# Landmark attention in one list of steps, and delta's first inverse on VectorE

## The chip, the cores and the metric

The kernel runs on one core of a Trainium2 chip. The metric is the device time of one execution, in microseconds (us).

## The reference

A decoder of two layers on x (4 batches, 512 tokens, 512 channels): delta-rule attention, a selective scan, a feed-forward with sign weights, landmark attention, cross attention with rotary positions, a feed-forward with ternary weights. After each comes `x = layernorm(x + f(x))`. The change is in the fourth, and at one place in the first. Landmark attention has 32 heads of 16 channels, eight blocks of 64 tokens, and 4 landmarks a block, 32 in all:

```python
q, k, v = split_heads(x @ w_qkv + b_qkv); q, k = rope(q), rope(k)
out_local = masked_softmax(qb @ kb * scale, causal) @ vb                # within each block of 64
lm = softmax(pool_q @ kb * scale) @ vb                                  # 4 landmarks per block
lm = lm + (masked_softmax(lq @ lk * scale, lm_mask) @ lv) @ w_lm_out    # lq, lk, lv = lm @ w_lm_qkv
lm = lm + (softmax((lm @ w_l2t_q) @ kb * scale) @ vb) @ w_l2t_out
gk, gv = lm @ w_lm_kv
out_global = masked_softmax(q @ gk * scale, g_mask) @ gv                # blocks before one's own
gate = sigmoid(x @ w_gate + b_gate)
out = ((1 - gate) * out_local + gate * out_global) @ w_out + b_out
```

In the delta rule each chunk of 32 tokens needs the inverse of a 32x32 unit triangular matrix for each head.

## The kernel before

Six stages run one after the other. Each has a class with a program for every engine: `pe_` TensorE, `act_` ScalarE, `dve_` VectorE, `pool_` GpSimd, `sp_` the queue of SyncE that issues most DMAs. The programs are in order and meet by semaphores. A stage starts when the stores of the one before have landed. A `Ring` hands out PSUM banks in a written order: TensorE fills a bank when the engine that read its last content has emptied it.

`Landmark` (line 1884) runs its four batches in a hardware loop, one turn each, with one set of buffers. All weights are loaded once, 3 MB of `wqkv` before the first product. A turn has four phases. The front: transposing x, the gate, v, q and k by token tile (`pe_project`, line 217), the rotation of q and k on VectorE (five operations each for q and k in each of four tiles, lines 2481 to 2491), and their transposes on TensorE (line 2215), copied by ScalarE. Then SyncE duplicates v into `VV` with 16 DMAs. The local phase: 16 items (c, t), eight heads and 128 tokens each, in the order of `local_order`. For an item GpSimd spreads the keys over eight masked copies `Kz` (line 2052), TensorE makes the scores (line 2237), VectorE adds the causal mask (line 2578), takes the maximum (2386) and subtracts it (2388), ScalarE takes exp (2349), VectorE sums (2498), TensorE transposes (2244), ScalarE copies, TensorE multiplies with v (2255). Between the items stand the 16 steps of the landmark `CHAIN`, whose small products, softmaxes and sums depend on each other. The global phase: eight items of 16 heads and 128 tokens against 32 landmark keys, the same way (lines 2267, 2637, 2366, 2608, 2274), and 32 narrow value products (line 2281); `mix` applies sums and gate on VectorE, and GpSimd scales the local part (2058). Output: 16 transposes (2289), the product with `wo` (224), residual, bias and normalization (2651 to 280), store. The next turn's x is loaded ahead, nothing else of it starts early.

`Delta` (line 343) works on eight pairs of batch and head half. For each, `pool_all` (line 531) inverts the triangles with 62 operations on GpSimd (lines 542 and 544), widths from 31 to 256, 10,912 columns in all, between the DMA that brings `p32` and the DMAs that carry the result to `DT`, which TensorE's triangle products wait for (line 623). Its ring has six banks; in its order V (two banks) stands six places before PT, the masked query product, and PT before the next pair's k products (line 606). GpSimd's operation for the next pair waits until the inverse before it is stored.

## Time and profile before

| what | value |
|---|---|
| median of 3 runs | 3782.99 us (3773.44 to 3783.01) |
| profiled execution: its own time, its span | 3802.12 us, 3800.4 us |
| busy in the span: TensorE, VectorE, ScalarE, GpSimd | 77%, 61%, 32%, 29% |
| mean granted clock of TensorE | 0.851 |
| landmark attention | 1943.1 to 2874.4 us, 931.3 us |

A row of a window gives its length, then for each engine its busy microseconds and, in brackets, its instructions; PEclk is TensorE's granted clock as a share of 2.4 GHz. PE is TensorE's products, PEld its weight loads, DVE VectorE, ACT ScalarE, POOL GpSimd. In a timeline a row is start, length, engine, source line, operation and shapes, with the idle time before it and what ended that. One f32 product shows as two records.

### The profile page before, as it was taken

Reading aid. Unit: us, or ns where it says so; the run is one execution under the profiler, and the core shown is the slowest. Engines: PE = TensorE matmul, PEld = TensorE weight load, DVE = VectorE, ACT = ScalarE, POOL = GpSimd, SP = SyncE. Lnnn points to the kernel's source line nnn. Section 1 sums busy time; section 2 is a strip of 40 time slices with the busy share of each in tenths; the row PEclk is TensorE's granted clock in tenths of the full one; section 3 lists DMA queues with packets and bytes.
Section 4 is the critical chain, followed back from the end, with each engine's and each line's share of the span. In section 5 each row is a group of like instructions: output and inputs, shape, how many; then the busy total and the mean of one; then the engine's idle time right before and its main releaser. Section 6 shows DMA issues by size and latency. Waiting matters only on the chain.

```text
span 3800.4 us, 53319 instructions
## 1 busy us (share of the span) xinstructions
PE 2924.6 (77%) x20710; PEld 1523.5 (40%) x20710; DVE 2317.4 (61%) x3434; ACT 1231.3 (32%) x2016; POOL 1104.5 (29%) x1044
## 2 busy tenths in 40 slices
PE   5788888765655655599968788878875798989877
PEld 4565656531222212244434545545452233333234
DVE  1233333327898989787727668575773565656567
ACT  3232323203434343211102212122121465645645
POOL 4433333305555555300002112020213442433000
PEclk8788988866877778899988788887887899999989
DMA  2222121103112120401050000000004543434211
GB/s 76 66 45 66 45 66 45 43 29 119 52 54 68 55 68 32 160 35 38 27 196 7 23 23 23 23 13 23 12 13 111 107 103 77 105 73 87 84 42 45
DMA packets 195820, 226.10 MB, mean 59 GB/s; under 512 B 99480, under 2 KB 131768, under 8 KB 194672
## 3 DMA queue, kind: packets, MB, share of 16 engines
q1 hardware_dynamic: 194480, 218.44, 20.4%
q0 software_dynamic: 1088, 4.19, 0.4%
q8 instruction: 171, 2.80, 0.3%
q14 instruction: 81, 0.66, 0.1%
HBM read 154.69 MB, written 54.92 MB: 55 GB/s over the span
## 4 chain that ended last, share of the span: by engine, by line
PE 39%; DVE 12%; issue 6%; ACT 3%; DMA 1%; SPq 0%; POOL 0%; DVEq 0%; ACTq 0%; POOLq 0%
PE ps L224 7%; PE ps L1726 4%; PE ps L1737 4%; PE ps L3007 3%; PE ps L2994 3%; PE ps L2980 2%; PE ps L2939 2%; PE ps L2971 2%; PE ps L2237 1%; DVE arena L2386 1%; PE ps L2281 1%; PE ps L2102 1%; DVE arena L1334 1%; PE ps L2255 1%; ACT arena L3085 1%
## 5 line engine op out<-in xcount | busy, mean ns | idle before, releaser
L3180 DVE TENSOR_REDUCE arena<-ps 128x1 f32<-128x512 f32 x512 | 330.7, 686 | 262.2 <-PE ps L2980 261.0
L224 PE MATMUL ps<-arena 128*128 128x512 f32 (+3 forms) x1296 | 478.2, 527 | 9.9 <-ACT arena L856 3.1
L1382 PE MATMUL ps<-arena 128*128 128x512 f32 x512 | 314.4, 759 | 129.9 <-POOL arena L1366 129.9
L1366 POOL TENSOR_TENSOR arena<-arena 128x1024 f32<-128x1024 f32 x128 | 309.6, 2419 | 299.3 <-DVE arena L1358 298.3
L3085 ACT ACTIVATE arena<-ps 128x512 f32<-128x512 f32 x512 | 288.1, 598 | 285.9 <-PE ps L2994 282.4
L1358 DVE TENSOR_TENSOR_SCAN arena<-ps,arena 128x1024 f32<-128x1024 f32 x128 | 291.7, 2280 | 64.2 <-ACT ps L1349 63.7
L2052 POOL TENSOR_TENSOR arena<-arena 128x1024 f32<-128x1024 f32 x64 | 127.3, 1994 | 605.5 <-ACT arena L2310 356.7
L224 PEld LDWEIGHTS ps<-arena 128*128 128x128 f32 (+2 forms) x1296 | 198.9, 157 | 255.9 <-issue 191.7
L542 POOL TENSOR_TENSOR arena<-arena 128x31 f32<-128x31 f32 (+15 forms) x248 | 149.0, 601 | 378.2 <-DMA arena<-d_a 359.4
L1382 PEld LDWEIGHTS ps<-arena 128*128 128x128 f32 x512 | 115.4, 239 | 320.7 <-POOL arena L1366 190.4
L1349 ACT ACTIVATE ps<-arena 128x511 f32<-128x511 f32 x256 | 165.2, 680 | 241.2 <-DVE arena L1358 241.0
L2994 PE MATMUL ps<-arena 99*128 99x512 bf16 x512 | 197.9, 389 | 54.4 <-ACT arena L3085 33.3
L2980 PE MATMUL ps<-arena 96*128 96x512 bf16 x512 | 199.1, 391 | 22.4 <-issue 18.1
L1726 PE MATMUL ps<-arena 128*128 128x512 bf16 x768 | 168.2, 381 | 7.7 <-issue 7.7
L1737 PE MATMUL ps<-arena 128*128 128x512 bf16 x768 | 166.9, 379 | 0.0
L1334 DVE TENSOR_TENSOR arena<-ps,arena 128x1024 f32<-128x1024 f32 x128 | 154.4, 1207 | 0.8
L1030 DVE TENSOR_TENSOR arena<-ps,arena 128x256 f32<-128x256 f32 x120 | 51.0, 425 | 165.4 <-PE ps L743 165.4
L3007 PE MATMUL ps<-arena 128*32 128x512 f32 x1024 | 141.6, 626 | 1.0 <-ACT arena L3085 1.0
L544 POOL TENSOR_TENSOR arena<-arena 128x31 f32<-128x31 f32 (+15 forms) x248 | 135.4, 546 | 19.4
L2994 PEld LDWEIGHTS ps<-arena 99*128 99x128 bf16 x512 | 49.5, 98 | 206.0 <-ACT arena L3085 142.9
L2878 POOL TENSOR_TENSOR arena<-arena 128x512 f32<-128x512 f32 x32 | 40.8, 1274 | 308.5 <-ACT arena L3058 308.5
L1378 PE MATMUL ps<-arena 128*128 128x512 f32 x32 | 32.6, 1123 | 114.2 <-DVE arena L1408 114.2
(337 smaller groups left out, 5421.7 us busy)
## 6 DMA issues: line engine op xcount, KB each, us to landing
arena<-d_bc SPq DMA_DIRECT2D x32, 1024.0 KB, 5.3
arena<-d_x SPq DMA_DIRECT2D x24, 1024.0 KB, 5.6
arena<-d_parts SPq DMA_DIRECT2D x192, 128.0 KB, 4.3
d_x<-arena SPq DMA_DIRECT2D x64, 256.0 KB, 2.5
d_parts<-arena SPq DMA_DIRECT2D x32, 384.0 KB, 2.4
arena<-arena SPq DMA_DIRECT2D x64, 128.0 KB, 2.0
d_w<-arena SPq DMA_DIRECT2D x3, 1408.0 KB, 4.8
arena<-d_w SPq DMA_DIRECT2D x3, 1408.0 KB, 11.2
```

The source lines that it names most:

```text
L224: ins = pe.e.matmul(ps[:m, :n], lhsT(k), rhs(k), start=(k == 0), stop=(k == chunks - 1))
L1334: dve.e.tensor_tensor(s.h[:, i % s.HS].rearrange("p (w l) -> p w l", w=s.W), spread(s.ps[:, s.DTU, :], 1, s.W), s.bc[:, turn % s.SLOTS, 0] ...
L1358: dve.e.tensor_tensor_scan(h, s.dA[:, i % 2].rearrange("p w l -> p (w l)"), h, 0.0, ALU.mult, ALU.add).then_inc(*dve.up("scan_scanned"))
L1366: pool.e.tensor_tensor(h, h, s.bc[:, turn % s.SLOTS, 1], ALU.mult).then_inc(*pool.up("scan_hC"))
L1382: ins = pe.e.matmul(y, s.ident, s.h[:, i % s.HS, w * L:(w + 1) * L], start=False, stop=last)
L1726: ins = e.matmul(ps, s.up[:, k, m * P:(m + 1) * P], s.xp[i][:, k, :], start=(k == i == 0), stop=(k == C - 1 and i == 2))
L1737: ins = e.matmul(ps, s.hp[i][:, m, t * P:(t + 1) * P], s.down[:, m, :], start=(m == i == 0), stop=(m == s.FC - 1 and i == 2))
L2980: pe.e.matmul(s.rmax.bank((u, m)), s.Qs[:s.N, slot, h, t * P:(t + 1) * P], s.Ks[:s.N, slot, h, :], start=True, stop=True).then_inc(*s.rmax ...
L2994: pe.e.matmul(s.rexp.bank((u, i)), s.Ks[:s.N + 3, slot, s.G * g + j, k * P:(k + 1) * P], s.Qs[:s.N + 3, slot, s.G * g + j, :], start=True, ...
L3007: ins = e.matmul(ps[32 * j:32 * j + 32, :], s.V[:, u % s.SLOTS, k, s.G * g + j, :], s.E[:, k % 2, j, :], start=(k == 0), stop=(k == s.KEYS ...
L3085: act.e.activation(s.E[:, k % 2, j], s.rexp.bank((u, i)), ACT.Exp).then_inc(*s.rexp.empty(act, (u, i)))
L3180: dve.e.tensor_reduce(s.mx[:, u % 2, t, h:h + 1], s.rmax.bank((u, m)), AX.X, ALU.max, negate=True).then_inc(*s.rmax.empty(dve, (u, m)))
```

## The change

The loop goes. `schedule` writes one list of steps for all four batches, and every engine's program walks that list: a first front; then for each batch 20 local steps, 11 global ones and four of output. Into the steps go the landmark chain, now 18 pieces, and the front of the next batch. v, QT, KT and the gates have two buffers, p has three. Weights other than wq and wk pass through three slots of 1 MB, loaded in the order of use.

q and k are computed transposed, 128 channels by 512 tokens (`r`), so that their transposes go. ScalarE adds the bias while copying; two DMAs swap neighbouring channels; GpSimd rotates with three operations of 512 columns. The local and global masks are bf16 products of an identity with the mask, accumulated under the scores, and VectorE's mask additions go. The masked keys are eight ScalarE copies of 128 columns an item, with a scale from memory. Sum and gate are applied to the exp before its transpose: VectorE makes a factor an item, GpSimd multiplies. The values are made transposed: v times the 64 transposed columns for the local part, eight products of 512 columns for the global part, added on VectorE; the output transposes go. v is duplicated whole by four DMAs of 512 KB, and GpSimd masks the pairs. In delta VectorE makes the inverse of the first pair; GpSimd keeps the other seven.

```diff
-        for n in range(s.PAIRS):
-            if n:
-                pool.e.wait_ge(*pool.on("delta_t32_out", n - 1))
+        for n in range(1, s.PAIRS):
+            pool.e.wait_ge(*pool.on("delta_t32_out", n - 1))
             e.tensor_tensor(s.t32, s.id32, s.id32, ALU.mult).then_inc(*pool.up_step("delta"))
             pool.e.wait_ge(*pool.on("delta_p32", n))
...
+    def dve_inverse(self, dve):
+        s, e, st = self, dve.e, "delta"
+        e.tensor_copy(s.t32, s.id32).then_inc(*dve.up_step(st))
+        dve.e.wait_ge(*dve.on("delta_p32", 0))
+        for j in range(s.Q - 1):
+            a, m = j + 1, s.Q - 1 - j
+            pr = s.prod[:, :a * m].rearrange("p (c i) -> p c i", i=m)
+            dve.e.wait_ge(*dve.at_step(st))
+            e.tensor_tensor(pr, spread(s.t32[:, :a, j], 2, m), spread(s.p32[:, a:, j], 1, a), ALU.mult).then_inc(*dve.up_step(st))
+            dve.e.wait_ge(*dve.at_step(st))
+            ins = e.tensor_tensor(s.t32[:, :a, a:], s.t32[:, :a, a:], pr, ALU.subtract)
+            if j < s.Q - 2:
+                ins.then_inc(*dve.up_step(st))
+            else:
+                ins.then_inc(*dve.up("delta_inverse"))
...
                     if i == 1:
                         s.dve_beta_k(dve, n)
+                        if n == 0:
+                            s.dve_inverse(dve)
...
+    CHAIN = ["pool_s", "pool_T", "pool_v", "lq", "lk", "lv", "ls", "lpT", "lo", "loT", "lout", "l2q",
+             "read_s", "read_T", "read_v", "rout", "gk", "gv"]
     SMALL = ["lq", "lk", "lout", "l2q", "rout", "gk"]
+    MATRICES = {"lq": ("D_wlm", 0), "lk": ("D_wlm", 1), "lv": ("D_wlm", 2), "v": ("D_wqkv", 2), "lout": ("D_wlo", 0), "l2q": ("D_wl2q", 0),
+                "rout": ("D_wl2o", 0), "gk": ("D_wkv", 0), "gv": ("D_wkv", 1), "y": ("D_wo", 0)}
+    TURNED = [(c, w) for w in (1, 0) for c in range(C)]
+    FIRST_FRONT = [[("xT", 0)], [("xT", 1)], [("xT", 2)], [("xT", 3)], [("r", 0)], [("r", 1)], [("r", 2)], [("r", 3)], [("r", 4), ("gateT", 0)],
+                   [("v", 0), ("gate", 0)], [("v", 1)], [("v", 2)], [("v", 3)]]
+    FIRST_LOCAL = {-2: [("r", 5)], -1: [("r", 6)], 0: [("r", 7)]}
+    LOCAL_FRONT = {2: [("xT", 0)], 3: [("xT", 1)], 4: [("xT", 2)], 5: [("xT", 3), ("gateT", 0)], 6: [("v", 0), ("gate", 0)], 7: [("v", 1)],
+                   8: [("v", 2)], 9: [("v", 3)], 11: [("r", 0)], 12: [("r", 1)], 13: [("r", 2)], 14: [("r", 3)]}
+    GLOBAL_FRONT = {-1: [("r", 4)], 2: [("r", 5)], 5: [("r", 6)], 8: [("r", 7)]}
...
+    def schedule(self):
+        s = self
+        fronts = lambda table, k, b: [(what, b, i) for what, i in table.get(k, [])] if b < B else []
+        for k, front in enumerate(s.FIRST_FRONT):
+            yield "front", -1, k, None, [(what, 0, i) for what, i in front]
+        for b in range(B):
+            for k in range(-2, s.N + 2):
+                first = fronts(s.FIRST_LOCAL, k, 0) if b == 0 else []
+                yield "local", b, k, s.CHAIN[k + 1] if 0 <= k + 1 < len(s.CHAIN) else None, first + fronts(s.LOCAL_FRONT, k, b + 1)
+            for k in range(-2, s.NG + 1):
+                yield "global", b, k, None, fronts(s.GLOBAL_FRONT, k, b + 1)
+            for t in range(T):
+                yield "out", b, t, None, []
...
+    def sp_vv(self, sp, b):
+        s = self
+        sp.e.wait_ge(*s.ring.at_emptied(sp, ("v", b, T - 1)))
+        if b:
+            sp.e.wait_ge(*s.ro.at_filled(sp, ("o", b - 1, C - 1)))
+        for half in range(2):
+            for b2 in range(2):
+                sp.e.dma_start(s.VV[64 * half:64 * half + 64].rearrange("p (t b) d -> p t b d", b=2)[:, :, b2, :],
+                               s.v[64 * b2:64 * b2 + 64, b % 2]).then_inc(*sp.up("landmark_vdup", 16))
...
+    def sp_swap(self, sp, b, r):
+        s, j = self, b * len(self.TURNED) + r
+        sp.e.wait_ge(*s.ring.at_emptied(sp, ("r", b, r)))
+        if j >= 2:
+            sp.e.wait_ge(*sp.on("landmark_rot", j - 2))
+        for odd in range(2):
+            sp.e.dma_start(s.sw[odd::2, j % 2], s.raw[1 - odd::2, j % 2]).then_inc(*sp.up(f"landmark_swapped{j % 2}", 16))
...
+    def pool_scale(self, pool, b, i):
+        s, j = self, b * self.N + i
+        pool.e.wait_ge(*pool.on("landmark_factor", j))
+        p = s.p[:, i % 3].rearrange("p (h n) -> p h n", n=s.S)
+        pool.e.tensor_tensor(p, p, spread(s.ls[:, i % 3], 2, s.S), ALU.mult).then_inc(*pool.up("landmark_scaled"))
...
+    def pool_rope(self, pool, b, r):
+        s, e, j = self, pool.e, b * len(self.TURNED) + r
+        c, w = s.TURNED[r]
+        if j == 0:
+            pool.e.wait_ge(*pool.at_all("landmark_rope"))
+        pool.e.wait_ge(*s.ring.at_emptied(pool, ("r", b, r)))
+        if j:
+            pool.e.wait_ge(*pool.on("landmark_rot", j - 1))
+        e.tensor_tensor(s.m1, s.raw[:, j % 2], s.cos, ALU.mult).then_inc(*pool.up("landmark_cos"))
+        pool.e.wait_ge(*pool.on(f"landmark_swapped{j % 2}", j // 2))
+        e.tensor_tensor(s.sw[:, j % 2], s.sw[:, j % 2], s.sin, ALU.mult).then_inc(*pool.up("landmark_sin"))
+        pool.e.wait_ge(*pool.on("landmark_cos", j))
+        pool.e.wait_ge(*pool.on("landmark_sin", j))
+        if b >= 2 and r == 0:
+            pool.e.wait_ge(*s.ring.at_filled(pool, ("gs", b - 2, s.NG - 1)))
+        e.tensor_tensor((s.QT, s.KT)[w][:, b % 2, c], s.m1, s.sw[:, j % 2], ALU.add).then_inc(*pool.up("landmark_rot"))
...
+    def pool_all(self, pool):
+        s = self
+        turned = []
+        for phase, b, k, chain, front in s.steps:
+            if phase == "local":
+                if s.item(k + 1) is not None:
+                    s.pool_scale(pool, b, k + 1)
+            if phase == "global" and s.item(k + 1, s.NG) is not None:
+                s.pool_g_scale(pool, b, k + 1)
+            for fb, r in turned:
+                s.pool_rope(pool, fb, r)
+            turned = [(fb, r) for what, fb, r in front if what == "r"]
+            if phase == "local" and b == 0 and -1 <= k < T - 1:
+                for i in range(2):
+                    s.pool_pairs(pool, 0, 2 * (k + 1) + i)
+            if phase == "global" and k >= s.NG - 3 and b + 1 < B:
+                for i in range(2):
...
+    def pe_scores(self, pe, b, i):
+        s, e, R = self, pe.e, self.ring
+        c, t = divmod(i, T)
+        if t == 0:
+            pe.e.wait_ge(*pe.on("landmark_rot", b * len(s.TURNED) + C + c))
+        if b == i == 0:
+            pe.e.wait_ge(*pe.at_all("landmark_masks"))
+        pe.e.wait_ge(*pe.on("landmark_kz", b * s.N + i))
+        pe.e.wait_ge(*R.at_free(pe, ("s", b, i)))
+        ps = R.bank(("s", b, i)).rearrange("p (h k) -> p h k", h=s.HC)
+        for b2 in range(2):
+            at = t * P + 64 * b2
+            e.matmul(ps[64 * b2:64 * b2 + 64], s.identb[:, 64 * b2:64 * b2 + 64], spread(s.m_local, 1, s.HC), start=True, stop=False)
+            ins = e.matmul(ps[64 * b2:64 * b2 + 64], s.QT[:, b % 2, c, at:at + 64], s.Kz[:, i % 2, :, 64 * b2:64 * b2 + 64], start=False, stop=True)
+        ins.then_inc(*R.fill(pe, ("s", b, i)))
...
+    def pe_global(self, pe, b, k):
+        s, e, R = self, pe.e, self.ring
+        i = s.item(k + 2, s.NG)
+        if i is not None:
+            half, t = divmod(i, T)
+            if i == 0:
+                pe.e.wait_ge(*pe.on("landmark_kz2", b, 2))
+            pe.e.wait_ge(*R.at_free(pe, ("gs", b, i)))
+            ps = R.bank(("gs", b, i)).rearrange("p (c n) -> p c n", c=2)
+            for c in range(2):
+                e.matmul(ps[:, c, :].rearrange("p (h n) -> p h n", n=s.NL), s.identb, spread(s.m_gl[:, t], 1, s.HC), start=True, stop=False)
+                ins = e.matmul(ps[:, c, :], s.QT[:, b % 2, 2 * half + c, t * P:(t + 1) * P],
+                               s.kz[:, 2 * half + c].rearrange("p h n -> p (h n)"), start=False, stop=True)
+            ins.then_inc(*R.fill(pe, ("gs", b, i)))
...
+    def act_kz(self, act, b, i):
+        s = self
+        c, t = divmod(i, T)
+        if t == 0:
+            act.e.wait_ge(*act.on("landmark_rot", b * len(s.TURNED) + c))
+        if i >= 2:
+            act.e.wait_ge(*s.ring.at_filled(act, ("s", b, i - 2)))
+        elif b:
+            act.e.wait_ge(*s.ring.at_filled(act, ("go", b - 1, C - 1)))
+        for h in range(s.HC):
+            act.e.activation(s.Kz[:, i % 2, h], s.KT[:, b % 2, c, t * P:(t + 1) * P], ACT.Copy, scale=s.bm16[:, h:h + 1]).then_inc(*act.up("landmark_kz"))
...
+    def act_all(self, act):
+        s = self
+        for phase, b, k, chain, front in s.steps:
+            if (phase, k, b) == ("local", -2, 0) or phase == "out" and k == 1 and b + 1 < B:
+                s.act_kz(act, b if phase == "local" else b + 1, 0)
+                s.act_kz(act, b if phase == "local" else b + 1, 1)
+            if phase == "local" and k >= -1 and s.item(k + 3) is not None:
+                s.act_kz(act, b, k + 3)
+            if phase == "local":
+                if k == -2 and b:
+                    s.act_sqrt(act, b - 1)
+                if s.item(k) is not None:
+                    s.act_turned(act, b, k)
+                if s.item(k + 2) is not None:
+                    s.act_exp(act, b, k + 2)
+                if k >= 1 and (k - 1) % T == T - 1:
+                    s.act_out(act, b, (k - 1) // T)
+            if phase == "global":
+                s.act_global(act, b, k)
+            if chain:
+                s.act_landmarks(act, chain, b)
+            for what, fb, i in front:
+                s.act_front(act, what, fb, i)
+        s.act_sqrt(act, B - 1)
...
+    def dve_scores(self, dve, b, i):
+        s, e, R = self, dve.e, self.ring
+        name, j = ("s", b, i), b * s.N + i
+        dve.e.wait_ge(*R.at_filled(dve, name))
+        if j >= 2:
+            dve.e.wait_ge(*dve.on("landmark_p", j - 2))
+        if i < 2 and b:
+            dve.e.wait_ge(*dve.on("landmark_g_exp", b * s.NG - 1))
+        if j == 0:
+            dve.e.wait_ge(*dve.at_all("landmark_masks"))
+        sc = s.sc[:, i % 2]
+        s.dve_shift(dve, sc, R.bank(name), None, s.mx[:, i % 2, :s.HC], s.HC, s.S).then_inc(*R.empty(dve, name))
...
+    def dve_factor(self, dve, b, i):
+        s, e, st = self, dve.e, "landmark"
+        c, t = divmod(i, T)
+        j = b * s.N + i
+        dve.e.wait_ge(*dve.on("landmark_p", j))
+        if j >= 3:
+            dve.e.wait_ge(*dve.on("landmark_scaled", j - 3))
+        ls = s.ls[:, i % 3]
+        e.tensor_reduce(ls, s.p[:, i % 3].rearrange("p (h n) -> p h n", n=s.S), AX.X, ALU.add).then_inc(*dve.up_step(st))
+        dve.e.wait_ge(*dve.at_step(st))
+        if i == 0:
+            dve.e.wait_ge(*dve.on("landmark_gated", b))
+        e.scalar_tensor_tensor(ls, ls, s.EPS, s.rungated[:, b % 2, t, c * s.HC:(c + 1) * s.HC], ALU.max, ALU.mult).then_inc(*dve.up_step(st))
+        dve.e.wait_ge(*dve.at_step(st))
+        e.reciprocal(ls, ls).then_inc(*dve.up("landmark_factor"))
...
+        dve.e.tensor_copy(s.m_gl, s.masks).then_inc(*dve.up("landmark_masks"))
+        for phase, b, k, chain, front in s.steps:
+            if phase == "local":
+                if k == -2 and b:
+                    s.dve_scale(dve, b - 1)
+                if s.item(k + 1) is not None:
+                    s.dve_factor(dve, b, k + 1)
+                if s.item(k + 2) is not None:
+                    s.dve_scores(dve, b, k + 2)
+            if phase == "global":
+                s.dve_global(dve, b, k)
+            if phase == "out":
+                s.dve_y(dve, b, k)
+            if chain in ("pool_T", "read_T"):
+                s.dve_pool_weights(dve, chain, b)
+            if chain:
+                s.dve_landmarks(dve, chain, b)
+            for what, fb, i in front:
+                s.dve_front(dve, what, fb, i)
+            if chain in s.SMALL:
+                s.dve_small(dve, chain, b)
+        s.dve_scale(dve, B - 1)
...
```

## Rows read from the trace of the kernel before

**Rows 1.** The page of the profile, busy time by engine.

```profile
PE 2924.6 (77%) x20710; PEld 1523.5 (40%) x20710; DVE 2317.4 (61%) x3434; ACT 1231.3 (32%) x2016; POOL 1104.5 (29%) x1044
```

**Rows 2.** Windows: busy time by engine, granted clock, in five stretches.

```profile
1966.70:2025.00 58.30, 51.78 (x174) 26.36 (x174) 30.05 (x46) 7.95 (x13) 3.78 (x2) 0.91 0.48 172
2025.00:2131.30 106.30, 86.11 (x1218) 53.52 (x1218) 80.27 (x126) 26.52 (x56) 27.84 (x14) 0.85 0.04 12
2131.30:2176.00 44.70, 32.39 (x146) 27.71 (x144) 31.38 (x54) 11.93 (x21) 5.29 (x5) 0.70 0.08 24
2192.80:2418.50 225.70, 185.67 (x1570) 114.63 (x1571) 153.53 (x250) 47.57 (x92) 37.23 (x21) 0.83 0.07 20
2930.00:3300.00 370.00, 323.66 (x1572) 122.06 (x1573) 227.60 (x416) 190.36 (x352) 153.47 (x149) 0.93 0.47 100
```

**Rows 3.** Timeline of VectorE and GpSimd in one local item.

```profile
2082.34 0.69 DVE L2578 TENSOR_TENSOR arena<-ps,arena 128x512 f32<-128x512 f32 x1 [0.34 <-PE ps L2237]
2082.38 1.90 POOL L2052 TENSOR_TENSOR arena<-arena 128x1024 f32<-128x1024 f32 x1 [3.44 <-PE ps L2237]
...
2083.79 1.04 DVE L2388 TENSOR_TENSOR arena<-arena 128x512 f32<-128x512 f32 x1
...
2084.75 0.67 DVE L2498 TENSOR_REDUCE arena<-arena 128x8 f32<-128x512 f32 x1
```

**Rows 4.** Timeline of TensorE in one local item: first and last line of three.

```profile
2089.45 1.08 PE L2237 MATMUL ps<-arena 128*64 128x512 f32 x4
...
2091.04 0.91 PE L2255 MATMUL ps<-arena 128*64 128x32 f32 x16
```

**Rows 5.** Instruction groups of landmark attention, shapes apart: busy, mean ns, idle.

```profile
L2281 PE MATMUL ps<-arena 128*128 128x64 f32 x256 | 49.7, 376 | 3.2 <-ACT arena L2372 3.1
...
L2215 PE MATMUL ps<-arena 128*128 128x128 f32 x128 | 20.8, 300 | 22.9 <-DVE arena L2491 22.9
...
L2058 POOL TENSOR_TENSOR arena<-arena 128x512 f32<-128x512 f32 x16 | 18.2, 1169 | 109.5 <-ACT arena L2358 109.5
...
L2303 ACT ACTIVATE arena<-arena 128x128 f32<-128x128 f32 x4 | 1.2, 310 | 25.5 <-DVE arena L2469 25.5
```

**Rows 6.** Timeline of VectorE in the rotation of q and k.

```profile
2003.15 0.43 DVE L2487 TENSOR_TENSOR arena<-arena 128x256 f32<-128x256 f32 x1
2003.61 2.16 DVE L2489 TENSOR_TENSOR arena<-arena 128x256 f32<-128x256 f32 x1
```

**Rows 7.** Timeline of VectorE in the last output product and normalization.

```profile
2861.25 0.69 DVE L2651 TENSOR_TENSOR arena<-arena,ps 128x512 f32<-128x512 f32 x1 [1.29 <-PE ps L224]
...
2864.69 0.69 DVE L2651 TENSOR_TENSOR arena<-arena,ps 128x512 f32<-128x512 f32 x1 [1.29 <-PE ps L224]
...
2868.09 1.92 DVE L280 TENSOR_SCALAR arena<-arena 128x512 f32<-128x512 f32 x4
```

**Rows 8.** Timelines: a bf16 product; the starts of landmark attention and cross attention.

```profile
1699.66 24.55 PE L1726 MATMUL ps<-arena 128*128 128x512 bf16 x113
...
1965.35 0.58 DVE L2025 TENSOR_SCALAR arena<-arena 128x4 f32<-128x4 f32 x3 [25.01 <-DMA arena<-in_D_wqkv]
...
2888.48 2.04 PE L2929 MATMUL ps<-arena 32*128 32x512 f32 x2 [23.83 <-DMA arena<-in_E_wkv]
```

**Rows 9.** Instruction groups of two other stages, cross attention and delta.

```profile
L2878 POOL TENSOR_TENSOR arena<-arena 128x512 f32<-128x512 f32 x23 | 29.3, 1274 | 208.8 <-ACT arena L3058 208.8
...
L883 ACT ACTIVATE arena<-arena 128x512 f32<-128x512 f32 x24 | 15.3, 706 | 0.0
```

**Rows 10.** Timelines of GpSimd and TensorE around delta's first inverse.

```profile
58.76 0.25 POOL L542 TENSOR_TENSOR arena<-arena 128x31 f32<-128x31 f32 x1 [44.01 <-DMA arena<-d_a]
...
100.17 0.27 POOL L544 TENSOR_TENSOR arena<-arena 128x31 f32<-128x31 f32 x1
...
71.09 8.64 PE L606 MATMUL ps<-arena 128*128 128x256 f32 x32
108.31 3.56 PE L623 MATMUL ps<-arena 128*32 128x128 f32 x64 [28.57 <-DMA arena<-d_t]
```

1197 lines of the change are left out of this document (597 added, 600 removed).

## The prediction

> **What bounds the kernel now.** I read first the busy line of the page [rows 1]: no engine fills the span, TensorE is nearest with 77%. Then the table by stretch [rows 2], because the change rewrites one stage, landmark attention, from 1943.1 to 2874.4 us: 23.6 us of loading and four turns of 226 to 230 us. In a turn TensorE is busy 184 to 186 us, VectorE 154, ScalarE 48, GpSimd 37, the clock at 0.83 to 0.84. The first turn, cut by phase: 58.3 us of projections and rotations, 106.3 of local items, 44.7 global, 16.8 output product. Nothing of one batch overlaps the next, so each phase has its own limit. In the local phase VectorE is busy 80.3 of 106.3 us: an item costs it four operations from 2082.34 to 2085.42, 3.1 us, or 2.7 where GpSimd doesn't interfere [rows 3], with gaps 2.9, against 2.45 us of TensorE (2089.45 to 2091.95 less the overlap with what follows) [rows 4]. In the global phase TensorE works 32.4 of 44.7 us at clock 0.70 and waits for VectorE. So the stage loses its time by engines taking turns, not by one full engine.
>
> **What stays on TensorE.** Per batch, full clock: a 512-column f32 projection of four products costs 3.43 us (two reads of its result, 2861.25 and 2864.69 [rows 7]). There are 18: v 4, q and k 8, y 4, two landmark values. All stay. The 32 q/k transposes go (20.8/4 = 5.2 us), so do the 16 of the mixed output (2.6 at the same price) and the 32 narrow value products of the global phase (49.7/4 = 12.4) for eight wide ones, 8 x 0.86 = 6.9 [rows 5]. The masks come in as 32 bf16 products of 512 columns and 16 of 256. In bf16 113 of 512 take 24.55 us, 0.217 each [rows 8]. Two at half width may run together, as the four f32 records of an item seem to do (1.08 us, where four of 0.43 in series would be 1.7 [rows 4]). So 0.22 to 0.43 an item; I take 0.4, 6.4 a batch, and 2 for the global ones. TensorE's sum is thus nearly unchanged: -20 + 15 = -5 us.
>
> **What leaves VectorE.** The rotation, eight times a batch five operations, three of 0.69 and two of 0.43 or, met by GpSimd, more [rows 6]: 24 to 27 us; the mask additions, (16 + 8) x 0.72 = 17; the mixing, which becomes four additions, about 3; the bias, 3. What comes is one small multiply and reciprocal an item, 24 x 0.4 = 10. So VectorE falls from 154 to about 115 us a batch. An item costs it 3 x 0.72 + 0.45 = 2.6 us in place of 2.9.
>
> **What ScalarE and GpSimd get.** ScalarE: an operation of 128 columns takes 0.310 us [rows 5]; one of 512 with a scale read from memory, as the masked copies have, 0.706, or 15.3/24 = 0.64 to the next [rows 9]. So I put a masked copy at 0.31 to the next, 2.5 us an item (bounds: a quarter of the wide one, 8 x 0.16, and as dear as the wide one, 8 x 0.64), nearest to the row of its own width, 40 us a batch. With exp, copies and eight rotation inputs it has about 90 us of a turn. GpSimd loses all it does now, 37 us [rows 2], and gets 24 scalings of 1.17 (the same shape with a spread operand), 8 rotations of three at 1.27, 8 pair maskings of 1.17, four biases: 28 + 30.5 + 9.4 + 4.7 = 73 us [rows 5, 9]. Neither is full at a turn near 190.
>
> One collision is real. A 256-column VectorE multiply with both inputs in SBUF takes 0.43 us, the next of its kind 2.16 when it meets GpSimd's key multiply [rows 6]. In a local item the subtraction, then in place in SBUF, takes 1.04 in place of 0.69, because GpSimd's multiply runs until 2084.28 [rows 3]. After the change only the tiny factor multiply of each item, 24 a batch, has two such inputs on the path; GpSimd runs 73 of 190 us, and what is met has about half of 1.2 us left: 24 x 0.38 x 0.6 = 5.5 us, of which VectorE's slack takes more than half (bounds 0 and 5.5). I put 2 on the path. The Trainium skill (SBUF — State Buffer, on the shared port pair) says that of such a pair the second to issue is fully blocked until the first ends, and that a VectorE operation with one SBUF input isn't touched. By that rule the shift from PSUM, which the change makes of every item, is free of it; the trace agrees, the addition from PSUM took 0.69 beside the same GpSimd multiply [rows 3].
>
> **The middle batches**, walked step by step, each step's base being 2.45 + 0.4 = 2.85 us of TensorE:
> Steps -2 to 1: nothing covers the turn of a batch. VectorE needs 5.3 us from the last y to the end of the normalization (2864.69 to 2870.01 [rows 7]), then 1.5 shift, 0.8 exp, 1.3 factor, 1.3 scale: 10.2 until the first transpose can start. Steps 0 and 1 are bound by VectorE's pool softmax and sums, 2.6 + 1.7 to 3.5 and TensorE's 4.3 of pooling products, 13 us. 23 us.
> The chain pieces below are counts of instructions at the price of their kind, estimates. Steps 2 to 9: eight bases 23, chain 10.7, tokens, gate and v 18.3, three handoffs of 1 us at the small transposes: 55 us.
> Steps 10 to 14: 13 of base, 9.5 of chain, four rotation inputs 13.7, 6 waiting for VectorE's l2z, weights and k: 42 us. The last two 8 us.
> So local 128 us, in which 32 us of the next batch's front are done. That TensorE's chain is near 40 us checks with [rows 2]: 86.1 busy less 16 x 2.45 is 47 at clock 0.85.
> Global: eight items at 3.7 us, since VectorE waits about 1 us for each exp before its sum (0.72 x 2 + 1 + 1.2), plus filling and draining: 40 us, with four rotation inputs (13.7) inside. Output: 4 x 3.43 + 2 = 16.
> Clock: TensorE busy near 90% of these phases should sit near the 0.93 it shows in the cross stage from 2930 to 3300 us [rows 2], not 0.83; that still costs 8 on 128. Sum 128 + 40 + 16 + 8 + 2 = **194 us** against 226.
>
> **Ends of the stage.** The first product waits now for 5.5 MB (VectorE idle 25.0 us for the last weight, 1965.35 [rows 8]). Afterwards it waits for x, k's weight and small tables, 2.1 MB with more behind them in the queue. The next stage's start is such a case: its first product comes at 2888.48, 14 us after the stores landed at 2874.4 [rows 8]. Bounds 10 and 16; I take 12.6, 11 saved. The first front stands alone: 36.6 us of products and 3.4 at low clock, 40. Its rotation swaps queue behind 5 MB of loads, up to some 1973 us, and five rotations of 3.8 end by 1992, just before the front does. The last batch has no front: steps of VectorE (2.6 plus a mean chain of 2.1) and handoffs, 98 local, 37 global, 16 output, 6 clock, 10 until stored: 167 us. Stage: 12.6 + 40 + 3 x 194 + 167 = 802 for 931: **-130 us**.
>
> **Delta's first inverse.** GpSimd works from 58.76 to 100.44, and TensorE sits 28.57 us idle for its result, which lands at 108.31, 7.9 after the inverse [rows 10]. On VectorE 256 columns take 0.43 [rows 6] and 512 0.69 [rows 3], so 0.16 us and 0.26 for each 256 columns, with 0.035 between; the 62 operations have 10,912 columns: 62 x 0.195 + 11.1 = 23.2 us, 18 sooner, landed at 90. But VectorE now takes V only after the inverse, at 83. The six-bank ring gives V's bank to PT, the masked query product (some 4.5 us of TensorE, an estimate: half of what follows), and behind that in TensorE's order are the next pair's k products, 8.6 us [rows 10]. So the triangles start near 96.5 instead of 108.3: 11.8, less 0.8 of low clock, **-11 us** (bounds: 0 and -18).
>
> **Sum.** -141 on the profiled execution's 3802.1 (span 3800.4) is 3661; that execution lies 19 above the median, so **3642 us** against 3782.99.
>
> **Rivals.**
> A: all handoffs are hidden. A batch costs TensorE's sum, about 178, at clock 0.97. For it: the cross stage holds 0.93 with TensorE 87% busy [rows 2]. Against: step -2 has nothing to hide in. 3 x 16 + 10 more saved: 3584.
> B: GpSimd paces. In the global phase a rotation of 3.8 us stands before the next scaling, and swaps wait for the 2 MB duplication of v; if scalings are late by 3.5 us in seven of the steps, 25 us a batch are lost in the three batches that have a next one: 3717. For it: GpSimd has 9.4 of scaling, 11.4 of rotation and 9.4 of pair masks in these 40 us. Against: the masks come last, behind most scalings.
> C, slower: ScalarE paces the local steps. Its program puts eight copies before each exp, and VectorE's sum waits on that exp. At 0.31 a copy the step needs 2.5 + 0.5 + 0.6 + 0.8 = 4.4 us, less than the mean step's 128/20 = 6.4. It turns slower when a batch grows by 141/4 = 35 us, 2.5 in each of the 14 steps with copies: a step of 8.9, copies of 0.87 us, dearer than the wide row. With 0.95 the step is 9.5, 43 a batch, the time 3814. The Trainium skill (ScalarE: Activation LUTs, rules for kernel authors) would have plain multiplies on VectorE; its cost with a pointer operand gives, as an estimate, 0.39 us a copy, and then the step has 5.0 us and nothing changes.
> D: delta's inverse brings nothing, because V blocks TensorE as long: 3653; inside the range.
>
> **Chances.** Forecast (with D) 0.56, own range 3605 to 3685; A 0.17; B 0.20; C 0.05; no change 0.02. The range reaches from A to B: 3575 to 3722, leaving out some 2 in 10. A difference under 0.3% of 3783, 11 us, can't be told from none here. Faster 0.93, same 0.02, slower 0.05.
>
> **What would show it.** Right: 12 to 14 us from the last store of the stage before to the first transpose; y products of two batches some 194 us apart; VectorE near 115 and GpSimd near 73 us busy a batch; clock over 0.9 in local steps; triangles of the first pair near 96 us, inverse operations on VectorE together 23 us. Wrong: transposes that wait for GpSimd's scaling in local steps (B), VectorE's sums that wait for exp over 2 us (C), or swaps landing 10 us after issue, which would hold the first batch.

## The result, and the profile after

The kernel after takes 3642.62 us (median of 4 runs, 3635.61 to 3648.05); the kernel before took 3783.0 beside it. The ratio is 0.9631, 95% interval 0.9605 to 0.9658. The profiled execution took 3648.05 us, span 3645.8, clock 0.869.

The page of the profile after, busy line, answers to [rows 1]: VectorE gives up 143 us, ScalarE gets 143, GpSimd 91.

```profile
PE 2822.2 (77%) x20518; PEld 1411.1 (39%) x20518; DVE 2174.3 (60%) x3357; ACT 1374.3 (38%) x2467; POOL 1195.2 (33%) x1137
```

The table by stretch of the kernel after. The cuts lie within 0.3 us of the first score product of each batch and at the last store, so that each of the four rows is one batch of landmark attention; the second and third answer to the middle turn of [rows 2].

```profile
1964.20:2170.30 206.10, 174.04 (x1546) 92.62 (x1547) 112.71 (x205) 84.59 (x206) 91.71 (x77) 0.89 0.32 97
2170.30:2362.20 191.90, 159.06 (x1523) 84.56 (x1521) 110.92 (x214) 83.91 (x205) 70.79 (x60) 0.91 0.30 94
2362.20:2556.60 194.40, 164.00 (x1521) 87.65 (x1519) 110.84 (x214) 83.92 (x205) 70.81 (x60) 0.88 0.29 93
2556.60:2719.00 162.40, 119.46 (x1374) 67.78 (x1370) 105.53 (x217) 68.89 (x175) 30.53 (x28) 0.83 0.19 66
```

Read a row in two parts: TensorE's busy time, and the rest, in which it stands. The middle turn before had 225.7 us, 185.67 of them busy at 0.83, so 40.0 idle. The two rows here have 32.8 and 30.4 idle. Busy time times the row's mean clock is an estimate of the work at full clock: 154.1 before, 144.7 and 144.3 now. A batch's 33 us are therefore about 8 of idle time, 11 to 12 of work taken off TensorE (9.6 at full clock), and the rest the same work at 0.91 or 0.88 in place of 0.83.

The stage's beginning, TensorE's timeline. It answers to [rows 8].

```profile
1925.45 3.65 PE L2252 MATMUL ps<-arena 128*128 128x128 f32 x16 [17.99 <-DMA arena<-in_c_group]
1929.78 19.44 PE L224 MATMUL ps<-arena 128*128 128x512 f32 x40 [0.69 <-ACT arena L2494]
...
1964.20 0.41 PE L2394 MATMUL ps<-arena 128*64 128x512 bf16 x2
1964.44 1.03 PE L2395 MATMUL ps<-arena 128*64 128x512 f32 x4
```

The stage starts at 1915.6 and its last stores end at 2719.0: 803.4 us, 127.9 less than before. VectorE's output additions (line 2849) begin at 2159.92, 2351.74, 2546.17 and 2701.48: the middle batches lie 191.8 and 194.4 us apart, the last 155.3 behind them. One mask pair costs 0.24 us, from 1964.20 to 1964.44.

The turn of a batch, TensorE's timeline and then VectorE's, of the turn at 2170 us. The first row holds five products of eight records: the next batch's last q projection and the four of the output.

```profile
2152.85 17.33 PE L224 MATMUL ps<-arena 128*128 128x512 f32 x40
...
2171.43 1.03 PE L2395 MATMUL ps<-arena 128*64 128x512 f32 x4
2172.39 1.06 PE L2313 MATMUL ps<-arena 128*32 128x512 f32 x8
2179.11 0.65 PE L2394 MATMUL ps<-arena 128*64 128x512 bf16 x2 [5.66 <-ACT arena L2536]
2179.54 1.92 PE L2395 MATMUL ps<-arena 128*64 128x512 f32 x4
2181.39 1.12 PE L2403 MATMUL ps<-arena 128*128 128x128 f32 x4
2184.54 0.66 PE L2319 MATMUL ps<-arena 128*128 128x128 f32 x4 [2.03 <-DVE arena L2672]
```

```profile
2172.82 1.92 DVE L280 TENSOR_SCALAR arena<-arena 128x512 f32<-128x512 f32 x4
2174.65 0.69 DVE L2654 TENSOR_REDUCE arena<-ps 128x8 f32<-128x512 f32 x1
2175.37 0.69 DVE L2656 TENSOR_TENSOR arena<-ps,arena 128x512 f32<-128x512 f32 x1
2176.76 0.69 DVE L2803 TENSOR_REDUCE arena<-arena 128x8 f32<-128x512 f32 x1 [0.69 <-ACT arena L2545]
```

Between the first score product of a batch and its first transposes 11.3 us pass (2170.11 to 2181.39). The wait of 5.66 us is put down to ScalarE's masked key, but that copy stands behind an exp which waits for VectorE's subtraction at 2175.37, and this for the normalization. The last 2.3 us before the transposes are the third score product itself: it stands ahead of them in TensorE's order and runs at a granted clock of 0.50, after 5.66 us in which TensorE stood (1.92 us, where the second took 1.03 at full clock).

Delta's first inverse, VectorE's and TensorE's timelines, and the chief waits of TensorE up to the triangles. They answer to [rows 10].

```profile
71.22 0.59 DVE L916 TENSOR_TENSOR arena<-arena 128x256 f32<-128x256 f32 x1
71.85 0.42 DVE L918 TENSOR_TENSOR arena<-arena 128x256 f32<-128x256 f32 x1
...
85.10 1.28 DVE L1016 TENSOR_TENSOR arena<-ps,arena 128x512 f32<-128x512 f32 x2
```

```profile
85.92 3.64 PE L674 MATMUL ps<-arena 128*32 128x128 f32 x64 [20.88 <-DVE arena L1016]
89.50 7.73 PE L605 MATMUL ps<-arena 128*128 128x256 f32 x32
97.15 1.95 PE L622 MATMUL ps<-arena 128*32 128x128 f32 x64
```

The inverse runs from 58.20 to 85.19. TensorE waits 20.88 us for V's banks, as the prediction had it, and the triangles start at 97.15. But the issue of delta's last stores went from 830.09 to 804.73, 25.4 us, where the prediction gave the whole edit 11. This, and whether each walked step had the bound that the prediction gave it, is what the experiments ask.

### The profile page after: what moved, and what is told of

The parts are those of the page before. It is cut to its first block, busy times and chain, and to the rows that moved or that the text cites. A ratio compares the mean times of both kernels' runs of the same rounds, so it can differ in the third digit from the quotient of the medians.

```text
span 3645.8 us, 51631 instructions
## 1 busy us (share of the span) xinstructions
PE 2822.2 (77%) x20518; PEld 1411.1 (39%) x20518; DVE 2174.3 (60%) x3357; ACT 1374.3 (38%) x2467; POOL 1195.2 (33%) x1137
## 4 chain that ended last, share of the span: by engine, by line
PE 40%; DVE 9%; issue 5%; ACT 3%; POOL 2%; DMA 1%; SPq 0%; ACTq 0%; DVEq 0%; POOLq 0%
PE ps L224 8%; PE ps L1745 5%; PE ps L1756 5%; PE ps L3238 4%; PE ps L3225 3%; PE ps L3211 3%; PE ps L3170 2%; PE ps L3202 2%; PE ps L2395 1%; PE ps L2452 1%; PE ps L2403 1%; DVE arena L1353 1%; ACT arena L3316 1%; PE ps L2296 1%; PE ps L3176 1%
## 5 line engine op out<-in xcount | busy, mean ns | idle before, releaser
L224 PE MATMUL ps<-arena 128*128 128x512 f32 (+3 forms) x1296 | 488.6, 533 | 8.4 <-ACT arena L855 3.2
L1401 PE MATMUL ps<-arena 128*128 128x512 f32 x512 | 312.8, 755 | 130.6 <-POOL arena L1385 130.6
L1385 POOL TENSOR_TENSOR arena<-arena 128x1024 f32<-128x1024 f32 x128 | 309.4, 2418 | 298.2 <-DVE arena L1377 297.1
L3225 PE MATMUL ps<-arena 99*128 99x512 bf16 x512 | 198.0, 389 | 54.5 <-ACT arena L3316 33.2
L541 POOL TENSOR_TENSOR arena<-arena 128x31 f32<-128x31 f32 (+15 forms) x217 | 130.0, 599 | 329.1 <-DMA arena<-d_a 312.7
L2159 POOL TENSOR_TENSOR arena<-arena 128x512 f32<-128x512 f32 x64 | 66.7, 1042 | 320.1 <-DVE arena L2809 320.1
L2536 ACT ACTIVATE arena<-arena 128x128 f32<-128x128 f32 x512 | 155.3, 388 | 0.0
L3109 POOL TENSOR_TENSOR arena<-arena 128x512 f32<-128x512 f32 x32 | 40.7, 1272 | 305.9 <-ACT arena L3289 305.9
L3225 PEld LDWEIGHTS ps<-arena 99*128 99x128 bf16 x512 | 49.5, 98 | 206.1 <-ACT arena L3316 142.6
```

The lines of the kernel that those rows point to most:

```text
L224: ins = pe.e.matmul(ps[:m, :n], lhsT(k), rhs(k), start=(k == 0), stop=(k == chunks - 1))
L1385: pool.e.tensor_tensor(h, h, s.bc[:, turn % s.SLOTS, 1], ALU.mult).then_inc(*pool.up("scan_hC"))
L1401: ins = pe.e.matmul(y, s.ident, s.h[:, i % s.HS, w * L:(w + 1) * L], start=False, stop=last)
L3225: pe.e.matmul(s.rexp.bank((u, i)), s.Ks[:s.N + 3, slot, s.G * g + j, k * P:(k + 1) * P], s.Qs[:s.N + 3, slot, s.G * g + j, :], start=True, ...
```

## Experiments

The kernel before was run beside each experiment. It took 3783.0 us beside the kernel after and beside e1 to e4, but 3777.0 beside e5 to e8, 3771.1 beside e9 to e11 and 3772.8 beside the last. Differences to the kernel after are given as differences of medians; from e5 on they are uncertain by these 6 to 12 us, and the ratios to the kernel before are the better measure.

### Delta: 11 or 25 us

The first kernel is the one before with the inverse of pair 0 on VectorE, the second the one after without it:

```diff
e1, in the kernel before (e2 is the reverse, in the kernel after)
-        for n in range(s.PAIRS):
+        for n in range(1, s.PAIRS):
...
                         s.dve_beta_k(dve, n)
+                        if n == 0:
+                            s.dve_inverse(dve)
```

> The kernel before, with delta's first inverse on VectorE and nothing else of the change. Theory 1 (clock): the move by itself brings what the prediction gave it, 11 us, up to the first pair's triangles (near 97 us in place of 108.3), and the later pairs keep their lag of 11 us; the 25.4 us that delta's last store moved in the profile after (830.09 to 804.73) are 14 us of other clock in later pairs (the last stretch held 0.79 in place of 0.69). Then the median falls by 11 us, and the last store lies anywhere within some 7 us of 819. Rival (queue): GpSimd or SyncE, free of the first inverse, lets each later pair start sooner; then every execution shows the last store near 805, and the median falls by 25 us.

> The kernel after, with delta's first inverse back on GpSimd. Theory 1 (clock): the first triangles return to 108.3, the median is 11 us above the kernel after, 3654. Rival (queue): 25 us above it, 3668. That both experiments on delta must agree tells the effect of the edit from the scatter of a single execution.

e1: 3768.58 us, ratio to before 0.9959 (0.9945 to 0.9973), 14 us less, where 11 were expected. e2: 3662.32 us, ratio 0.9687 (0.9669 to 0.9705), 20 us over the kernel after. The traces: with GpSimd's inverse the first triangles start at 108.31 (before) and 110.16 (e2); in the ten kernels with VectorE's unchanged inverse (after, e1 and e4 to e11) between 97.0 and 99.8. So 11 to 13 us (108.31 to 97.03 in e1, 110.16 to 97.15 from e2) are the edit's. From these triangles to delta's last store it is 721.8 us before and 697.7 in e2, the same program; with VectorE's inverse 694.7 to 711.8, 703.3 in the mean of ten. The execution profiled before was the long one: in that stretch the same records of TensorE, 7,976 of them, were busy 588.1 us at a clock of 0.84, 577.2 at 0.86 in the kernel after and 571.0 at 0.87 in e2. Of the 14.2 us between before and after, 10.9 are thus clock and 3.3 idle time. In its last stretch of delta (742.90 to 830.10) the clock was 0.69, in the kernel after (722.30 to 804.70) 0.79, as these rows of the tables by stretch show, before and then after:

```profile
742.90:830.10 87.20, 61.23 (x808) 41.19 (x808) 24.11 (x54) 6.63 (x11) 0.00 (x0) 0.69 0.00 1
```

```profile
722.30:804.70 82.40, 56.53 (x808) 37.23 (x808) 24.07 (x54) 6.52 (x11) 0.00 (x0) 0.79 0.01 1
```

The queue theory, 25 us in every execution, falls: e1's interval is 10 to 21 us. The medians say 14 and 20 for an edit that moves the triangles by 11 to 13. Whether some of the 3 to 9 us beyond the forecast 11 belongs to the edit stays open.

```diff
e3, in dve_inverse, after column j's subtraction
+                if j in (8, 12):
+                    s.dve_beta_v(dve, 0, (j - 8) // 4)
```

> The kernel after; VectorE reads V's two banks in the middle of the inverse, after its 9th and 13th column, in place of after it. The prediction's step says that V keeps its banks until the inverse is done, so that the masked query product and the next pair's k products (11.3 us together) stand between inverse and triangles. If so, the query product now starts near 63 us in place of 85.92, and the triangles wait for the DMA of the inverse alone: V costs VectorE 1.3 us, the inverse lands near 94.5, the triangles start near 94.5 in place of 97.15, the median falls by 2.5 us. If V's banks do not hold TensorE, the query product stays near 86 and nothing moves.

3643.29 us, ratio 0.9632 (0.9617 to 0.9647): no difference that the times can show. TensorE's timeline of e3:

```profile
66.71 1.21 PE L674 MATMUL ps<-arena 128*32 128x128 f32 x32 [1.21 <-ACT arena L882]
70.32 1.94 PE L674 MATMUL ps<-arena 128*32 128x128 f32 x32 [2.41 <-DVE arena L1018]
72.19 8.23 PE L605 MATMUL ps<-arena 128*128 128x256 f32 x32
94.56 3.64 PE L622 MATMUL ps<-arena 128*32 128x128 f32 x64 [14.14 <-DMA arena<-d_t]
```

The query product starts 19 us sooner (at 66.71, where 63 was expected), the next pair's k products 17, and the triangles wait for the DMA alone and come at 94.56, as expected to a tenth. V's banks did hold TensorE. What they cost was 2.6 us, because behind them the inverse's DMA was nearly as late.

### The turn of a batch

```diff
e4, VectorE
-                if k == -2 and b:
-                    s.dve_scale(dve, b - 1)
...
                     s.dve_scores(dve, b, k + 2)
+                if k == -1 and b:
+                    s.dve_scale(dve, b - 1)
ScalarE
                     s.act_sqrt(act, b - 1)
+                if k == -2:
+                    s.act_kz(act, b, 2)
```

> The kernel after, with another order at the turn of a batch: VectorE takes the first two score items of the new batch ahead of the normalization's last scaling of the old one, and ScalarE makes the third masked key ahead of the first exp. In the profile after TensorE waits 5.66 us there for ScalarE's masked key, once in each of three turns. If the turn is paced as the prediction says, by VectorE's 5.3 us from the last y to the end of the normalization and the chain behind it, the first scores are shifted 2 us sooner and the wait falls to some 2 to 3 us: 3 us a turn, 9 us in all, 3634. If the wait only moves to the first transpose, which needs exp, factor and scaling in turn, 2 us a turn or less are left, 3637 to 3642; later stores of x may cost the next load nothing, since it is needed only four steps later.

3652.84 us, ratio 0.9661 (0.9647 to 0.9676): slower than the kernel after by 10 us, where 3 to 9 less were expected. TensorE and ScalarE in e4, at the turn at 2356:

```profile
2360.39 0.41 PE L2394 MATMUL ps<-arena 128*64 128x512 bf16 x2 [1.51 <-ACT arena L2536]
2360.62 1.03 PE L2395 MATMUL ps<-arena 128*64 128x512 f32 x4
2364.61 1.12 PE L2403 MATMUL ps<-arena 128*128 128x128 f32 x4 [2.95 <-POOL arena L2159]
2372.04 1.11 PE L2319 MATMUL ps<-arena 128*128 128x128 f32 x4 [6.32 <-DVE arena L2674]
```

```profile
2357.90 2.43 ACT L2536 ACTIVATE arena<-arena 128x128 f32<-128x128 f32 x8
2360.35 1.28 ACT L2545 ACT_TABLE_LOAD   x1
2361.64 0.63 ACT L2545 ACTIVATE arena<-arena 128x512 f32<-128x512 f32 x1
```

The key's wait fell from 5.66 to 1.51 us and the first transposes came 9.1 us after the first score product (2355.53) in place of 11.3. But VectorE now waits 3.2 us for an exp behind the copies and behind a table load that had run in idle time, and does its 1.92 us of scaling later: the pooling product starts 16.5 us after that score product in place of 14.4, and TensorE's idle time of a middle batch is 32.4 and 33.2 us, against 32.8 and 30.4 in the kernel after and 30.2 and 31.0 in e3, which has this stage unchanged. The wait named by the trace was a symptom. In the kernel after VectorE is idle for only 0.27 and 0.69 us from its last output addition at 2170.22 to the pooling weights at 2184.49, so its work up to there paces the turn. The two orders were changed together, and which of them costs how much stays open; so does a part of the 10 us, since three turns with 1 to 2 us more idle time each do not make them up.

```diff
e10, GpSimd, in place of VectorE's four
+            if phase == "local" and k == -2 and b:
+                pool.e.wait_ge(*pool.on("landmark_rstd", b - 1))
+                for t in range(T):
+                    pool.e.tensor_scalar(s.x[:, t, :], s.x[:, t, :], s.norm.mv[:, t, 0:1], s.norm.rstd[:, t:t + 1], ALU.subtract, ALU.mult)
```

> The kernel after; at the three inner turns of a batch GpSimd, idle for 15.45 us there, makes the normalization's last scaling (four operations of 512 columns) and VectorE (1.92 us of it) does not. Theory 1, after the experiment on the turn's order: VectorE is busy nearly all of the 15 us from the last output to the first pooling weights, so that the same work in another order gains nothing and work taken away gains all of its 1.9 us a turn: the first transposes and the pooling product start 1.9 us sooner after the last y product, 3643 - 5.7 = 3637. Rival: ScalarE's eight key copies (2.43 us) and table load pace the turn, then the third score product starts as late as now, 8.9 us after the first of the batch ends, and 3643 stays.

3642.32 us, ratio 0.9654 (0.9632 to 0.9675), where the kernel after has 0.9631 (0.9605 to 0.9658): no gain, where 5.7 us were expected. The third score product starts 7.1 us after the first (2359.86 to 2366.92; 9.0 in e3), so VectorE's part is as expected. GpSimd's isn't:

```profile
2362.63 8.25 POOL L2202 TENSOR_SCALAR arena<-arena 128x512 f32<-128x512 f32 x4 [10.37 <-DVE arena L2880]
2370.85 2.04 POOL L2159 TENSOR_TENSOR arena<-arena 128x512 f32<-128x512 f32 x2
```

Its four operations take 2.06 us each, and the first item's scaling, due at 2365.7, waits for them until 2370.85. The first transposes come 12.1 us after the first score product in place of 11.3; the pooling product still gains 0.8. VectorE's multiply for the pooling weights, both inputs in SBUF, takes 1.46 us beside GpSimd's scaling (2371.99), 0.69 in the kernel after.

### The local and global steps

```diff
e5, the list of steps ("r" is a q or k projection)
-                   8: [("v", 2)], 9: [("v", 3)], 11: [("r", 0)], 12: [("r", 1)], 13: [("r", 2)], 14: [("r", 3)]}
-    GLOBAL_FRONT = {-1: [("r", 4)], 2: [("r", 5)], 5: [("r", 6)], 8: [("r", 7)]}
+                   8: [("v", 2)], 9: [("v", 3)]}
+    GLOBAL_FRONT = {}
...
                 yield "out", b, t, None, []
+            if b + 1 < B:
+                for i in range(2 * C):
+                    yield "front", b, 20 + i, None, [("r", b + 1, i)]
```

> The kernel after, but the eight q and k products of the next batch and their rotations stand in eight steps of their own behind the output product of the batch before, not in its local and global steps; x, gate and v stay ahead. Theory 1, the prediction's walk: in local steps 11 to 14 the products are TensorE's own time, so that leaving saves 13.7 us there; in the global phase they lie in VectorE's shadow, so that leaving saves nothing; standing alone they cost 27.4 us and some 6 of the last swap and rotation. A middle batch then takes 194 - 13.7 + 27.4 + 6 = 214 us, the kernel 3643 + 3 x 20 = 3702. Rival (TensorE paces every step): order alone costs only the tail of 6 us, three times: 3661. Rival (GpSimd paces the global phase, B of the prediction): the phase also gets shorter by the three rotations that stood before scalings, 3690 or less.

3693.90 us, ratio 0.9781 (0.9739 to 0.9823), 51 over the kernel after, 59 expected. From one batch's first score product to its first global product the middle batches take 120.9 and 127.4 us (132.2 and 134.7 after), so local steps get 11 and 7 shorter where the walk gave 13.7. The global phase up to the row with the output product takes 39.5 in both (42.4 and 42.5 after, 39.4 and 39.2 in e3 with the same stage), so the three projections inside it cost nothing that stands out of that scatter, as the walk has it. But the fourth stands behind the last global product, in the row of the output product (17.33 us for five products), where nothing covers it: its 3.4 us are TensorE's own. Standing apart, the twelve products run in one row of 41.47 us, and the last rotation adds 3.2, not 6. A middle batch grew by 13 and 17 us, 20 expected.

```diff
e6, the local part (the global one likewise)
-            e.matmul(ps[64 * b2:64 * b2 + 64], s.identb[:, 64 * b2:64 * b2 + 64], spread(s.m_local, 1, s.HC), start=True, stop=False)
...
-        s.dve_shift(dve, sc, R.bank(name), None, s.mx[:, i % 2, :s.HC], s.HC, s.S)
+        s.dve_shift(dve, sc, R.bank(name), s.m_localf, s.mx[:, i % 2, :s.HC], s.HC, s.S)
```

> The kernel after, with the local and global masks added by VectorE again (one 512-column addition before each maximum, the subtraction then in place in SBUF) and not by TensorE. VectorE's sum rises by 24 x 0.72 = 17.3 us a batch, TensorE's falls by 16 x 0.24 + 16 x 0.11 = 5.6. Theory 1: VectorE sets the pace at the turn (four items) and in the eight global steps, so a middle batch gets 12 x 0.72 = 8.6 us longer, and the last batch, which has no front, by up to all 17: 3643 + 3 x 8.6 + 17 = 3686. Rival (TensorE paces everything): the products taken away show as a gain, 3643 - 4 x 5.6 = 3620. Rival (port): the subtraction in place has both inputs in SBUF again and meets GpSimd's scaling, which would add up to 24 x 0.35 us a batch: 3720.

3685.93 us, ratio 0.9760 (0.9717 to 0.9802): 3686 was expected. The four global phases grew by 4.2 to 6.2 us each (47.7, 46.6, 48.7 and 44.8, where they were 42.0, 42.4, 42.5 and 39.0), the local ones by 1.5 to 6.5. Eight additions of 0.72 are 5.8 us, so the global steps give back about the whole price: VectorE paces them. Of the sixteen additions in the local steps, 11.5 us, less than half shows in the mean. That the sum met 3686 is in part luck: a middle batch grew by 10.7 and 12.3 us where 8.6 were given, the last by 9.7 where it was 17.

```diff
e7, after the eight key copies of an item
+        for h in range(s.HC):
+            act.e.wait_ge(*act.on("landmark_kz", b * s.N + i, h + 1))
+            act.e.activation(s.Kz[:, i % 2, h], s.KT[:, b % 2, c, t * P:(t + 1) * P], ACT.Copy, scale=s.bm16[:, h:h + 1])
```

> The kernel after, with every masked key copied twice by ScalarE (the second eight copies write the same again), 16 x 2.43 = 39 us of ScalarE more a batch, at 0.606 us a copy in effect. Theory 1: ScalarE has 84 of 192 us to do and its copies are needed three steps ahead; only at the turn, where TensorE waits for the third key, do 2.4 us show, and perhaps twice: 3643 + 4 x 2.4 to 4.8, 3653 to 3662. Rival C of the prediction (ScalarE paces the local steps, since the copies stand before the exp that VectorE's sum waits for): it counted slack of 2 us in the mean step of 6.4; where steps are shorter than the mean each adds up to 2.4, 16 steps of it would be 39 us a batch, 3643 + 155 = 3798.

3663.50 us, ratio 0.9693 (0.9650 to 0.9736), 21 over the kernel after and just past the upper end of 3653 to 3662; 3798 was the rival's. ScalarE is busy 120 us of a middle batch of 195 to 197, in place of 84. The theory put 2.4 to 4.8 us at each turn. The first batch grew by 0.7, the middle ones by 5.6 and 0.6, and the last, whose local steps are shortest (102.4 us for twenty), by 13.5: there rival C's mechanism shows, for a third of its price. TensorE's waits for a key went from 17.3 us in 4 to 33.3 in 10.

```diff
e8, in place of the eight copies
+        pool.e.tensor_tensor(s.Kz[:, i % 2], spread(s.KT[:, b % 2, c, t * P:(t + 1) * P], 1, s.HC), spread(s.bm16, 2, P), ALU.mult)
```

> The kernel after, with the masked keys made by GpSimd again, one 1024-column multiply an item (1.90 us in the profile before), not by ScalarE. GpSimd gets 30 us more a batch, 71 + 30 = 101 of 192; ScalarE gets 39 less, 45. Theory 1: neither was full; the key of an item now stands behind the scaling of an earlier one, and each key blocks VectorE's factor multiply when they meet: at the turn some 2 us, and 16 x 0.5 x 0.5 = 4 us a batch of longer factor multiplies, half of it on the path: 3643 + 4 x 4 = 3659. Rival: the change needed ScalarE's help because GpSimd would pace the steps with rotations (1.04 + 1.9 + 3.8 = 6.7 us in steps 12 to 15): 5 us a step more there, 3643 + 3 x 20 + 16 = 3719. Rival: the copies on ScalarE cost something now, then it gets faster than 3635.

3668.52 us, ratio 0.9721 (0.9678 to 0.9764), 26 over the kernel after where 16 were expected. GpSimd's timeline in e8 at a turn, TensorE's there, and then both in the first batch:

```profile
2378.98 1.04 POOL L2159 TENSOR_TENSOR arena<-arena 128x512 f32<-128x512 f32 x1 [11.74 <-DVE arena L2809]
2379.98 1.90 POOL L2540 TENSOR_TENSOR arena<-arena 128x1024 f32<-128x1024 f32 x1
```

```profile
2381.93 0.64 PE L2399 MATMUL ps<-arena 128*64 128x512 bf16 x2 [7.46 <-POOL arena L2540]
```

```profile
1977.00 1.26 POOL L2178 TENSOR_TENSOR arena<-arena 128x512 f32<-128x512 f32 x1 [11.20 <-DMA arena<-arena]
...
1982.06 1.90 POOL L2540 TENSOR_TENSOR arena<-arena 128x1024 f32<-128x1024 f32 x1
```

```profile
1984.01 0.64 PE L2399 MATMUL ps<-arena 128*64 128x512 bf16 x2 [16.45 <-POOL arena L2540]
```

At a turn the third key now stands behind the first item's scaling and costs TensorE 7.46 us in place of 5.66. The larger price lies in the first batch. There a key stands behind a rotation whose channel swap is still being copied, and TensorE waits 16.45 us for it; that batch grew by 11.2 us and its idle time from 32.1 to 46.2. The local factor multiply kept its median of 167 ns, so the port wasn't the price.

```diff
e9, VectorE in a global step: this block moved ahead of the block with the factor of item k + 1
+        i = s.item(k + 2, s.NG)
+        if i is not None:
...
+            s.dve_shift(dve, sc, R.bank(name), None, s.mx[:, i % 2], 16, s.NL)
```

> The kernel after; in each global step VectorE shifts the next item ahead of the sum and factor of the item before, not behind them. In the last batch of the profile after a global step takes 3.15 us, of which VectorE waits 0.69 for the exp that it has itself only just released; the new order fills that wait with the next shift. Theory 1: VectorE paces this phase; a step falls to some 2.5 us in the last batch, 5.5 us less; in the three batches with q and k products inside TensorE has some 39 us of work in 42, so that 2 to 3 us each are left: 3643 - 5.5 - 7.5 = 3630. Rival (TensorE or GpSimd paces it): the wait moves, nothing is gained, 3643.

3663.15 us, ratio 0.9700 (0.9674 to 0.9726): 21 us slower than the kernel after, where 13 less were expected. The last batch's global phase, without projections, takes 38.9 us, as it does after (39.0) and in e3 (38.8): VectorE's waits for an exp went, 4.0 us, and waits for a score product came, 3.0 us. In the three batches with q and k projections it is 46.7, 46.3 and 46.3 us in place of 42.0 to 42.5. A shift needs a score product, and this stands in TensorE's order behind a projection of 3.43 us; now the factor, and so the next transposes, stand behind the shift too. In one middle batch VectorE waits 6.4 us in 4 for score products, where it was 3.2 in 1. VectorE paces the phase only as long as nothing of TensorE's is put into its loop.

```diff
e11, GpSimd (part 0 is the first operation of a rotation, part 1 the others)
             for fb, r in turned:
-                s.pool_rope(pool, fb, r)
+                s.pool_rope(pool, fb, r, 0)
...
+            for fb, r in half:
+                s.pool_rope(pool, fb, r, 1)
```

> The kernel after; each rotation's second and third GpSimd operation run one step later than its first, so that no scaling stands behind a whole rotation of 3.8 us or behind a swap that has not landed. Rival B of the prediction held that scalings late by rotations stretch the global phase. In the profile after TensorE waits in the global steps 6.6 us a batch for GpSimd's scaling where rotations run, and 11.7 us in the last batch, which has none. Theory 1: those waits are VectorE's pace seen through GpSimd; spreading gains at most the 1 to 2 us a batch by which a scaling stood behind a rotation: 3638 to 3643. Rival B: the waits go, 6 us in each of three batches: 3625.

3635.89 us, ratio 0.9632 (0.9608 to 0.9657), single executions from 3612 to 3642. The median is 7 us below the kernel after's, the ratio is the same, so that the times show no gain. Idle time of a middle batch is 29.2 and 29.7 us, 1.2 less than in e3 in the mean, and GpSimd doesn't set the global phase (39.1 and 39.3 us, as in e3). What it shows beside that is in the first batch, which fell from 206.1 to 195.8 us. GpSimd and TensorE in the kernel after:

```profile
1971.16 1.27 POOL L2176 TENSOR_TENSOR arena<-arena 128x512 f32<-128x512 f32 x1
1984.71 1.27 POOL L2178 TENSOR_TENSOR arena<-arena 128x512 f32<-128x512 f32 x1 [12.29 <-DMA arena<-arena]
1986.12 1.26 POOL L2183 TENSOR_TENSOR arena<-arena 128x512 f32<-128x512 f32 x1
1987.35 2.49 POOL L2193 TENSOR_TENSOR arena<-arena 128x512 f32<-128x512 f32 x2
1989.79 1.05 POOL L2159 TENSOR_TENSOR arena<-arena 128x512 f32<-128x512 f32 x1
```

```profile
1990.88 1.11 PE L2403 MATMUL ps<-arena 128*128 128x128 f32 x4 [6.38 <-POOL arena L2159]
```

GpSimd waits 12.3 us for the sixth swap. Its input was ready at 1969.8, it was issued at 1974.59, behind the duplication of v and the late weights (issued from 1965.03 on), and its two DMAs landed 8.9 and 9.4 us after their issue, where those of the third to fifth swap took 1.9 to 2.4. The second item's scaling stands behind it, and TensorE waits 6.38 us. In e11 this wait is gone and TensorE waits 2.60 and 2.64 us for two later scalings; the batch's idle time fell from 32.1 to 29.5 us, and the rest of its 10 us is a clock of 0.94 for 0.89, which is scatter.

### The three edits together

> The kernel after with three edits together: V's banks read inside delta's first inverse (the triangles came 2.6 us sooner with it), each rotation's second and third operation one step later (in the profile with it the first batch lost TensorE's wait of 6.4 us for a scaling that stood behind a swap 12.3 us late, and a middle batch 1.5 us of TensorE's idle time), and the inner turns' scaling on GpSimd (1.9 us of VectorE a turn). If they add up: 2.6 + 6.4 + 3 x 1.5 + 3 x 1.9 = 19 us below the kernel after, 3624. Rival: only the waits are gained that one sees in TensorE's own row (delta's 2.6 and the first batch's 6.4), and the rest hides elsewhere: 3634. A profile with a clock near 0.88 would give some 20 us less than one near 0.87, whatever the edits do, so that the idle times decide and not the single time.

3622.19 us, ratio to the kernel before 0.9607 (0.9581 to 0.9632). The median is 20 us below the kernel after's, where 19 were expected; by the ratios, 0.9607 and 0.9631, it is 9 us, and the intervals overlap. The rows of the first three batches:

```profile
1957.60:2151.50 193.90, 164.77 (x1547) 86.92 (x1545) 114.57 (x205) 84.58 (x206) 91.95 (x77) 0.95 0.34 103
2151.50:2341.90 190.40, 160.40 (x1523) 84.75 (x1521) 108.41 (x210) 84.09 (x205) 78.69 (x64) 0.90 0.30 95
2341.90:2529.70 187.80, 160.53 (x1521) 84.26 (x1519) 109.41 (x210) 84.26 (x205) 78.49 (x64) 0.90 0.30 96
```

Idle time is 29.1, 30.0 and 27.3 us, against 32.1, 32.8 and 30.4 after. That is 9 us, and the first triangles start at 94.01, 3.1 us sooner. These 12 us, and the 9 of the ratios, lie nearer to the rival's 9 than to the 19 of the theory: the rest of the 20 is clock, and that the kernel before, too, was 10 us faster beside these runs. That the three gains add up is not shown.

## Why the prediction was right

**The sum.** 3642 predicted, 3642.62 measured. The direction and the mechanism held; that it met to 1 us is luck, since terms that were 2 to 12 us off cancel. Against the profiled execution of before, 154.1 us went and 141 were forecast. The 13 too many are delta in that one execution, mostly its clock, and they fall out again because it lay 19 above its median, while the one of after lies 5 above. If delta's edit gave 14 to 20 us, as the medians of e1 and e2 say, the landmark stage gave correspondingly less than 130 in the medians; the runs don't settle that.

**Landmark attention**, 802 predicted, 803.4 measured, piece by piece. From the last store before it to the first transposes: 12.6 predicted, 9.85 measured. First front: 40, 38.75. Middle batches: 194, and 191.8 and 194.4. In them the local steps were given 128 and 8 of clock, together 136, and took 132.2 and 134.7; the global steps with four projections were given 40 and took 45.8 and 45.9, the fourth of them uncovered behind the last global product; output was given 16 and took 13.9. So the global term was 6 us too small and the other two as much too large. The walk's steps 10 to 14 also count 13 us for five bases of 2.85, which are 14.3. Last batch: 167, against 162.4.

**The first batch** is the term of this stage that was missized. It was counted as a middle one, 194, and took 206.1. Three projections of 3.43 us that the first front leaves over stand in its first steps, 10 us that the prediction's sum has nowhere: its TensorE work is 155 us at full clock, 10 more than a middle batch's. The swap that GpSimd awaits for 12 us made a wait of 6.4 there, which takes the place of a middle batch's wait at the turn; idle time is 32.1 us in all, about as in the middle ones. The prediction looked for late swaps in the first front, where five rotations do end in time; the sixth lies just behind it. Its own sign of being wrong, swaps landing 10 us after issue, nearly came (8.9 and 9.4 us), and it held the first batch as said, for those 6.4 us. Most of the 12 us was made good by the stage's start (3), the first front (1), the last batch (5) and the two middle ones (2).

**TensorE's work.** -5 predicted at full clock, -9.6 measured. The masks cost 0.24 us an item and not 0.4, since the two halves of a pair start within 0.01 us of each other; that is 2.6 of the 4.6 us, no run shows where the rest lies. The clock over a middle batch is 0.88 and 0.91, short of the 0.93 taken from the cross stage; over its local steps it is 0.91 and 0.86, so that the sign "over 0.9" came in one of the two. The two errors offset each other.

**The other engines** a batch: VectorE 115 predicted, 111 measured; ScalarE 90, 84; GpSimd 73, 71. A key copy is 0.303 us to the next (155.3 us for 512 of them), 0.31 predicted from a row of its width. The Trainium skill (ScalarE: Activation LUTs, rules for kernel authors) would have put the copies on VectorE. No run tried that. Each copy by itself takes 0.387 us. The Trainium skill (ScalarE: Activation LUTs, What ACT_TABLE_LOAD costs) gives 0.39 with a pointer operand, as an estimate, and the trace agrees. Rival C is wrong: with twice the copies the kernel took 3664.

**The collision** has the right size and half the right place. The prediction took the factor multiplies to be the only operations on the path with two SBUF inputs. The 64 local ones keep 0.167 us in the median (five are longer, up to 0.526). But of the 32 global ones nine, three in each batch that has a next one, meet an operation of a rotation and take 0.73 to 0.93 us in place of 0.175, in the kernel after:

```profile
2313.77 0.92 DVE L2828 SCALAR_TENSOR_TENSOR arena<-arena 128x16 f32<-128x16 f32 x1
```

```profile
2313.39 1.27 POOL L2178 TENSOR_TENSOR arena<-arena 128x512 f32<-128x512 f32 x1
```

That is 2.0 us a batch of VectorE time in all factor multiplies; how much of it is on the path no run shows. The larger collision was left out: it sits in the four multiplies that spread the landmark queries, which meet GpSimd's four bias additions.

```profile
2253.44 4.65 DVE L2718 TENSOR_TENSOR arena<-arena 128x256 f32<-128x256 f32 x4
```

```profile
2252.28 5.52 POOL L2216 TENSOR_TENSOR arena<-arena 128x512 f32<-128x512 f32 x4
```

The shortest of these multiplies takes 0.424 us, the median 1.48, and TensorE waits 2.9 us a batch for the last. The price put on the path, 2 us, was of this size, but for another operation. The prediction's words that a VectorE operation with one SBUF input isn't touched are too wide: the 512-column copy of line 2730, from SBUF to SBUF, takes 0.43 us by itself and 1.52 beside a rotation's multiply (at 2296.38). The Trainium skill (SBUF — State Buffer, on the shared port pair) has the one fully blocked until the other ends, which the trace agrees with: each multiply takes as long as one of GpSimd's additions, 1.44 in the median.

**Handoffs at the turn.** 10.2 us were given from the last output product to the first transposes; it is 11.3 (2170.11 to 2181.39). The chain itself was shorter than said: the first item's scaling ends at 2179.00, 8.8 us after the last output addition starts. The 2.3 us of the third score product, which the walk left out here, make up for it. e4 and e10 show that the chain runs through VectorE, ScalarE and GpSimd. Rival A, which hid it all, missed by 58 us.

**Delta.** Inverse on VectorE 23.2 predicted, 27.0 measured: the multiply with two spread inputs takes 0.59 us at 256 columns, the subtraction 0.42. The 0.43 of [rows 6] was right for one of the two. Triangles at 96.5 predicted, 97.15 measured. V's banks held TensorE as said, and rival D is wrong.

**Rival B**, GpSimd's lateness in the global steps, is wrong for the three batches that it named (e11: their global phases are those of e3), and its mechanism right for one place of the first batch.

## What to carry to other kernels

A walk through the programs of all engines, step by step with measured durations, gave a restructured stage to 0.2%, with errors of single phases up to 6 us that cancel; what it missed most was the first pass, whose contents and DMA queue differ from the steady state, so walk that by itself. A wait that the trace names need not be the pace: two reorderings aimed at named waits (e4 and e9) cost 10 and 21 us, since an operation that was moved ahead took what it waits for into another engine's loop. Where single executions scatter, compare TensorE's idle time and its busy time times clock, and judge an edit of 10 us by those; they scatter too (the unchanged middle batches have 30.2 to 32.8 us of idle time in the kernel after, e2 and e3). Compare kernels by their ratio to one that ran beside them: the medians said 20 us for the three edits, the ratios 9.

## What was unexpected of the hardware

GpSimd takes 2.06 us for a 512-column subtraction and multiplication with one value a partition, and 1.04 us for a 512-column multiply of two tensors of which one is spread. The same delta program took 722 us in one execution and 698 in another from its first triangles on; in a stretch of 87 us the granted clock was 0.69, in the like stretch of the kernel after 0.79. Two bf16 products that each load 64 columns of weights and stream 512 leave only 0.24 us to the next instruction (1964.20 to 1964.44), little more than the 0.217 of a single one with 128 [rows 8], though each record is 0.40 us long. A VectorE multiply of 16 columns, 0.175 us by itself, took up to 0.93 beside one of GpSimd.
